# A recurrence's attention weights written already transposed, and its gate products in three pieces

## What is computed

```python
def step(h, x_t):
    proj = h @ W
    score = jnp.einsum('bsh,bh->bs', enc_hiddens, proj)
    attn = jax.nn.softmax(score, axis=-1)
    context = jnp.einsum('bs,bsh->bh', attn, enc_hiddens)
    inp = jnp.concatenate([x_t, context], axis=-1)
    gx = inp @ kernel + bias
    gh = h @ recurrent_kernel
    ...
    z = jax.nn.sigmoid(xz + hz)
    r = jax.nn.sigmoid(xr + hr)
    cand = jnp.tanh(xh + r * hh)
    h_new = z * h + (1.0 - z) * cand
```

## Time and profile before

| | |
|---|---|
| median of 3 runs | 3105.05 us (3101.61 to 3105.86) |
| span of the profiled execution | 3108.8 us |
| TensorE busy | 2731.3 us, 88% |
| VectorE busy | 2144.2 us, 69% |
| ScalarE busy | 1712.7 us, 55% |
| GpSimd busy | 995.6 us, 32% |

### The profile page before, as it was taken

One profiled execution on the slowest core, in us unless ns is written; L12 is line 12 of the kernel. 1 busy time (PEld: TensorE's weight loads), 2 busy tenths in 40 slices (PEclk: granted clock), 3 DMA queues, 4 the chain that ended last, 5 costly groups with the idle time before them and its releaser, 6 DMA issues. The chain is left out here.

```text
span 3108.8 us, 131004 instructions
## 1 busy us (share of the span) xinstructions
PE 2731.3 (88%) x54162; PEld 1800.4 (58%) x54163; DVE 2144.2 (69%) x8143; ACT 1712.7 (55%) x5762; POOL 995.6 (32%) x1992
## 2 busy tenths in 40 slices
PE   7999999887877999898999898999989877777768
PEld 4666666575455555565666565666656544444438
DVE  5666666773433888688888688777868766776653
ACT  4666666533443666576766576666657543333322
POOL 2000000230100666355666355555535311000015
PEclk9999999999878999999999999999999999999989
DMA  4000000000011000010000010000001000000013
GB/s 141 5 5 7 5 5 5 11 1 4 16 37 35 7 14 31 3 38 10 11 10 31 3 44 4 10 7 11 27 3 37 4 3 3 3 4 3 4 45 80
DMA packets 41078, 56.49 MB, mean 18 GB/s; under 512 B 6238, under 2 KB 27688, under 8 KB 40360
## 3 DMA queue, kind: packets, MB, share of 16 engines
q1 hardware_dynamic: 36392, 42.46, 4.3%
q0 software_dynamic: 4096, 5.67, 0.9%
HBM read 42.45 MB, written 5.67 MB: 15 GB/s over the span
## 5 line engine op out<-in xcount | busy, mean ns | idle before, releaser
L2183 POOL TENSOR_TENSOR gru_terms<-gru_states,gru_signs 128x8 f32<-128x8 f32 x512 | 104.2, 203 | 1180.9 <-DVE gru_states L2470 1077.7
L2103 ACT ACTIVATE gru_p<-gru_ps_sg,gru_negmax 128x78 f32<-128x78 f32 x512 | 167.5, 327 | 355.6 <-DVE gru_negmax L2439 350.4
L2107 ACT ACTIVATE gru_th_r<-gru_pre_r 128x32 f32<-128x32 f32 x512 | 118.8, 232 | 406.7 <-DVE gru_pre_r L2450 406.7
L1691 PE MATMUL gru_ps_sg<-ctx_gate_w,gru_p_t 128*4 128x64 f32 x12288 | 268.4, 221 | 0.1
L368 ACT ACTIVATE self_probs<-self_sc,self_negmax 128x512 f32<-128x512 f32 x256 | 174.4, 685 | 166.1 <-DVE self_negmax L425 166.1
L1936 PE MATMUL gru_ps_sg<-score_w,gru_states 128*4 128x78 f32 x4096 | 165.5, 234 | 94.3 <-DVE gru_states L2470 93.4
L2159 POOL TENSOR_SCALAR bg_probs<-bg_probs,bg_arsum 128x256 f32<-128x256 f32 (+2 forms) x192 | 241.0, 1255 | 19.0
L2443 DVE STREAM_TRANSPOSE gru_p_t<-gru_p 128x96 f32<-128x96 f32 x512 | 142.7, 279 | 112.1 <-ACT gru_p L2103 111.9
L2439 DVE TENSOR_REDUCE gru_negmax<-gru_ps_sg 128x1 f32<-128x78 f32 x512 | 121.7, 238 | 135.4 <-PE gru_ps_sg L1936 132.0
L1940 PE MATMUL gru_ps_own<-late,gru_states 128*4 128x128 f32 x4096 | 208.7, 276 | 0.0
L1691 PEld LDWEIGHTS gru_ps_sg<-ctx_gate_w,gru_p_t 128*4 128x4 f32 x12288 | 172.9, 86 | 38.4 <-issue 0.3
(11 more groups left out here) (421 smaller groups left out, 7391.5 us busy)
## 6 DMA issues: line engine op xcount, KB each, us to landing
bg_w<-in_moe_w SPq DMA_DIRECT2D x48, 256.0 KB, 2.9
bg_wa<-in_wqkv SPq DMA_DIRECT2D x24, 192.0 KB, 2.3
moe_w<-in_moe_w SPq DMA_DIRECT2D x16, 256.0 KB, 2.9
best_w_sb<-in_ec_w SPq DMA_DIRECT2D x16, 256.0 KB
cross_scratch<-ctab_raw SPq DMA_DIRECT2D x16, 154.0 KB
cross_outs<-cross_scratch POOLq DMA_DIRECT2D x4, 576.0 KB, 6.1
late<-in_late SPq DMA_DIRECT2D x1, 2269.5 KB
self_w_sb<-in_wqkv SPq DMA_DIRECT2D x8, 192.0 KB, 2.4
```

What stands on the lines that cost most here:

```text
L1691: last = pe.matmul(bank[32 * c:32 * c + B, 0:hi - lo], p_t[:, 32 * k:32 * k + B], gate_w[:, k, 96 * c + lo:96 * c + hi], start=k == 0, sto ...
L2103: act.activation(p[:, 0:CTX + 1], ps_s[:, 0:CTX + 1], ACT.Exp, bias=negmax[:, 0:1], accum_out=total[:, 0:1])\
```

## The change

The scores are computed a second time, with keys on partitions and the 12 pairs (chunk of keys, batch) as columns (`ps_t`), onto a mask product that leaves each block of partitions its own batch. The first set of scores is written to all 32 partitions of a batch, and is used only for the maximum. The exponential reads `ps_t` and writes `p_t`, the operand of the gate products, itself; the transposition, the sum of the exponential, `spread` and the products with it go. `gate_w` gets two columns of ones behind the 32 columns of r in each chunk, so that the product for r also gives the sum; its reciprocal is taken after that product. r with the sum, c and z are three groups of products. The wait for the old-state terms and the history copy moves from the last scan to the transposition of z.

With it the background is dealt out anew: TensorE issues all of it in one place, `after_gates`, between the products for z and the next step's x products; the halves of `down` and of the gate biases become one; the x products wait for `pre_z`; there are three fills in a step without background instead of eight. `STAGES` and the offsets are set anew, q/k transposes always go to a half of `bk_out`, and the pieces of ScalarE and VectorE change places around the recurrence's instructions. The output weights of a head pair have their own semaphores (`s_wo`) and are loaded later than its projections.

The diff, cut to its core:

```diff
--- before.py
+++ after.py
+                dve.scalar_tensor_tensor(out=by_chunk[:, :, 0:32], in0=bias[:, :, 0:32], scalar=is_key[:, k:k + 1],
+                                         in1=product[:, :, 0:32], op0=ALU.mult, op1=ALU.add)
+                dve.scalar_tensor_tensor(out=by_chunk[:, :, GATE_C:GATE_ALL], in0=bias[:, :, 32:96], scalar=is_key[:, k:k + 1],
+                                         in1=product[:, :, 32:96], op0=ALU.mult, op1=ALU.add)
+                dve.tensor_copy(by_chunk[:, :, 32:GATE_C], is_key[:, k:k + 1].rearrange("p (a b) -> p a b", a=1).broadcast_to([P, 4, 2]))
...
-        ps_sg, ps_own, ps_tz = pb("ps_sg"), pb("ps_own"), pb("ps_tz")
-        ps_s, ps_g, ps_t, ps_z = ps_sg[:, 0:P], ps_sg[:, P:2 * P], ps_tz[:, 0:P], ps_tz[:, P:2 * P]
...
+        ps_sr, ps_tc, ps_oz = pb("ps_sr"), pb("ps_tc"), pb("ps_oz")
+        ps_s, ps_r, ps_total = ps_sr[:, 0:CTX + 1], ps_sr[:, P:P + GATE_C], ps_sr[:, P + 32:P + 33]
+        ps_t, ps_c = ps_tc[:, 0:3 * B], ps_tc[:, P:P + 32]
+        ps_own, ps_z = ps_oz[:, 0:P], ps_oz[:, P:P + 32]
...
+        STAGES = {2: {"project": 0, "squares": 0, "take_v": 1, "sums": 1, "scales": 1, "rows": 2, "turn": 2, "take_qk": 4, "scores": 5,
+                      "max0": 6, "exp0": 6, "max1": 7, "exp1": 7, "scale0": 7, "scale1": 8, "probs0": 7, "probs1": 8, "turned0": 7, "turned1": 9,
+                      "values": 9, "take_out": 10, "out": 10, "add": 11},
+                  3: {"project": 0, "squares": 0, "take_v": 1, "sums": 1, "scales": 1, "rows": 2, "turn": 2, "take_qk": 4, "scores": 4,
+                      "max0": 5, "exp0": 5, "max1": 6, "exp1": 6, "scale0": 6, "scale1": 7, "probs0": 7, "probs1": 8, "turned0": 8, "turned1": 9,
+                      "values": 9, "take_out": 10, "out": 11, "add": 12}}
...
-        STAGES = {2: {"project": 0, "squares": 1, "scales": 1, "rows": 2, "turn": 2, "scores": 3, "max0": 4, "exp0": 4, "max1": 5, "exp1": 5,
-                      "scale0": 5, "scale1": 6, "probs0": 6, "probs1": 7, "values": 8, "out": 9, "add": 10},
-                  3: {"project": 0, "squares": 1, "scales": 2, "rows": 3, "turn": 3, "scores": 4, "max0": 5, "exp0": 5, "max1": 6, "exp1": 6,
-                      "scale0": 6, "scale1": 7, "probs0": 7, "probs1": 8, "values": 8, "out": 9, "add": 10}}
...
-                        last = pe.matmul(bank[32 * c:32 * c + B, 0:hi - lo], p_t[:, 32 * k:32 * k + B],
-                                         gate_w[:, k, 96 * c + lo:96 * c + hi], start=k == 0, stop=k == 2,
+                        last = pe.matmul(bank[32 * c:32 * c + B, 0:hi - lo], p_t[:, B * k:B * k + B],
+                                         gate_w[:, k, GATE_ALL * c + lo:GATE_ALL * c + hi], start=k == 0, stop=k == 2,
...
-                for j in (2 * half, 2 * half + 1):
+                for j in range(B):
...
             def turn_qk(g, n, m):
                 pe.wait_ge(s_rows, m + 1)
-                if PACE[g] == 2:
-                    wait_positive(pe, s_add, m - 3)
-                else:
-                    wait_positive(pe, s_apte, 2 * (m - 2) + 2)
-                    wait_positive(pe, s_xt, turned)
+                wait_positive(pe, s_aq, m)
+                wait_positive(pe, s_oe, min(m - 3 if PACE[g] == 2 else m - 2, g * U))
+                if n < 4:
+                    wait_positive(pe, s_add, (g - 1) * U)
...
-            def after_own(t):
-                busy = False
-                for g, n, m in chunks_at(t, 4):
-                    down(g, n, m, 1)
-                    busy = True
-                for g, n, m in units_at(t, "turn"):
-                    turn_qk(g, n, m)
-                    busy = True
-                for j in range(2):
-                    for g, n, m in units_at(t, f"probs{j}"):
-                        turn_probs(g, n, m, j)
-                        busy = True
...
-                if not busy:
-                    wait_positive(pe, s_prez, t)
-                    fill_in(2 * P, ps_tz)
-
-            def before_scores(t):
+            def after_gates(t):
                 busy = False
                 for g, n, m in chunks_at(t, 0):
                     up(g, n, m)
                     busy = True
                 for g, n, m in chunks_at(t, 3):
-                    down(g, n, m, 0)
+                    down(g, n, m)
+                    busy = True
+                for g, n, m in units_at(t, "turn"):
+                    turn_qk(g, n, m)
                     busy = True
                 for g, n, m in units_at(t, "project"):
                     project(g, n, m)
...
                     busy = True
+                for j in range(2):
+                    for g, n, m in units_at(t, f"probs{j}"):
+                        turn_probs(g, n, m, j)
+                        busy = True
...
             for t in range(S):
-                if t:
-                    pe.wait_ge(s_own, t)
+                busy = t and after_gates(t - 1)
+                wait_positive(pe, s_prez, t)
                 wait_positive(pe, s_xt, t // P)
                 for c in range(4):
                     pe.matmul(ps_own[32 * c:32 * c + B, 0:96], x_t[:, B * t:B * (t + 1)], x_w[:, c, :], start=True, stop=False,
                               tile_position=(0, 32 * c), skip_group_check=True)
-                busy = t and before_scores(t - 1)
-                wait_positive(pe, s_u, t)
-                pe.matmul(ps_s[:, 0:CTX + 1], mask_l, mask_r[:, 0:CTX + 1], start=True, stop=False, skip_group_check=True)
+                pe.matmul(ps_t, mask_l, mask_r, start=True, stop=False, skip_group_check=True)
                 if not busy:
-                    wait_positive(pe, s_prez, t)
-                    for i in range(6):
-                        fill_in(2 * P, ps_tz)
+                    for i in range(3):
+                        fill_in(2 * P, ps_sr)
                 pe.wait_ge(s_h, t + 1)
                 for b in range(B):
-                    last = pe.matmul(ps_s[32 * b:32 * b + B, 0:CTX + 1], state(t), score_w[:, b, 0:CTX + 1], start=False, stop=True,
-                                     tile_position=(0, 32 * b), skip_group_check=True)
+                    last = pe.matmul(ps_s[32 * b:32 * b + 32, :], state(t)[:, b:b + 1].broadcast_to([P, 32]), score_w[:, b, 0:CTX + 1],
+                                     start=True, stop=True, tile_position=(0, 32 * b))
                 last.then_inc(s_score, 1)
+                for k in range(3):
+                    for b in range(B):
+                        last = pe.matmul(ps_t[32 * b:32 * b + 32, B * k:B * k + B], score_w[:, b, 32 * k:32 * k + 32], state(t),
+                                         start=False, stop=True, tile_position=(0, 32 * b), skip_group_check=True)
+                last.then_inc(s_turnedmm, 1)
                 for c in range(4):
-                    last = pe.matmul(ps_own[32 * c:32 * c + B, 0:P], state(t), h_w[:, c, :], start=False, stop=True,
+                    last = pe.matmul(ps_own[32 * c:32 * c + B, :], state(t), h_w[:, c, :], start=False, stop=True,
                                      tile_position=(0, 32 * c), skip_group_check=True)
                 last.then_inc(s_ownmm, 1)
-                after_own(t)
                 pe.wait_ge(s_exp, t + 1)
-                for c in range(4):
-                    last = pe.matmul(ps_t[32 * c:32 * c + B, 0:2], spread, total[:], start=True, stop=True, tile_position=(0, 32 * c))
-                last.then_inc(s_total, 1)
+                gate_products(ps_r, 0, GATE_C).then_inc(s_rmm, 1)
+                gate_products(ps_c, GATE_C, GATE_Z).then_inc(s_cmm, 1)
                 pe.wait_ge(s_own, t + 1)
-                fill_in(P, ps_own)
-                pe.wait_ge(s_pt, t + 1)
-                gate_products(ps_g, 0, 64).then_inc(s_rcmm, 1)
-                pe.wait_ge(s_rt, t + 1)
-                gate_products(ps_z, 64, 96).then_inc(s_zmm, 1)
+                gate_products(ps_z, GATE_Z, GATE_ALL).then_inc(s_zmm, 1)
...
                 act.wait_ge(s_max, t + 1)
-                act.activation(p[:, 0:CTX + 1], ps_s[:, 0:CTX + 1], ACT.Exp, bias=negmax[:, 0:1], accum_out=total[:, 0:1])\
-                   .then_inc(s_exp, 1)
+                act.wait_ge(s_turnedmm, t + 1)
+                act.activation(p_t[:], ps_t, ACT.Exp, bias=negmax[:, 0:1]).then_inc(s_exp, 1)
...
+                        add_out(g, n, m)
+                for j in range(2):
+                    for g, n, m in units_at(t, f"max{j}"):
+                        maximum(g, n, m, j)
...
             for t in range(S):
                 before_maximum(t)
                 dve.wait_ge(s_score, t + 1)
-                dve.tensor_reduce(negmax[:], ps_s[:, 0:CTX + 1], axis=AX.X, op=ALU.max, negate=True).then_inc(s_max, 1)
+                dve.tensor_reduce(negmax[:], ps_s[:, 0:CTX], axis=AX.X, op=ALU.max, negate=True).then_inc(s_max, 1)
+                after_maximum(t)
                 dve.wait_ge(s_ownmm, t + 1)
```

(60 more changed lines are left out.)

141 lines of the change are left out of this document (60 added, 81 removed).

## The result

The changed kernel takes 3158.14 us (median of 4 runs, 3152.97 to 3167.19) against 3105.45 us (4 runs, 3101.61 to 3110.28) on the same chip: ratio 1.0179, 95% interval 1.0153 to 1.0204. It is 53 us slower; forecast were 93 us less, and the measured time lies outside the range (2920 to 3120).

What follows compares the result with a forecast made beforehand. Quiet steps were taken as bounded by the recurrence's chain, busy ones by TensorE's order. Tail -77 and +3, attention 3 -14, attention 2 +8, attention 1 -5, experts +4, remaining steps -13, setup +1: 3105 - 93 = 3012 us, range 2920 to 3120.

Steps and rivals of the forecast that it cites:

- The chain, part by part: Step without background, followed from the start of the score products: 3.76 falls by 0.55 to 3.21 us.
- (a): Scores to exponential: the 12 new turned products hide under the maximum; exponential starts at 0.69 us, against 0.66 today.
- (c): Gate products to pre_r: serial reciprocal costs 0.27, narrower first product gives 0.16 back; pre_r at 1.58 us; candidate's products cost nothing.
- The busy step: Steps with background, bounded by TensorE's order: with all background in one place, period 2.01 us plus the background's time.
- Rival 1: Turned products: 32-column loads run serially, exponential 0.44 us later in every step, +225, total 3237 us; chance 0.11.
- (b): Exponential on 12 columns instead of 78 takes 0.21 us; gate products at 0.95, against 1.44 today.
- (d): Last wait before the state scan: 0.04 instead of 0.14 us after the candidate's transposition, 0.10 saved.
- Expert step: Step with expert background: period 3.95 us against 3.91, +0.04.
- W: TensorE's time for the background in a busy step, between z and the next x products; 1.94 us with experts.
- Attention 2: Steps of the second background attention: 4.31 us with scores, 3.95 with projections, mean 4.13 against 4.01, +0.12.
- rival 2: Background steps: waits once met in two windows meet in one, +0.3 us a step, +99, total 3111 us; chance 0.12.
- Rival 4: Steps without background: fewer fills lower TensorE's granted clock, 0.3 us more a step, +42, total 3054 us; chance 0.15.

Runs made afterwards that it cites:

- experiment 2: Kernel before plus 24 unread small products a step where TensorE waits for the exponential: 3297.97 us; control with 3 fills instead: 3136.8; kernel before 3096.21.
- experiment 6: Changed kernel with candidate and z joined in one product, r with total apart: 3025.37 us, ratio 0.9734; also with the earlier background schedule: 2979.19, 0.959.
- experiment 1: Changed kernel with r, total and candidate as one product: 3071.62 us, ratio to the kernel before 0.9912; second run with z joined too: 3117.45, 1.0066.
- old schedule: Background placed as in the kernel before, half of it between own-state and gate products; on the changed kernel with candidate and z joined: 2979.19 us, ratio 0.959.
- the kernel with the fewest instructions: Changed kernel with r, total, candidate and z as one product 98 wide: 3117.45 us, ratio to the kernel before 1.0066.
- old schedule, three products: Changed kernel with the background schedule of the kernel before, r, candidate and z still three products: 3141.29 us, ratio to the kernel before 1.0136.

## Why the prediction was wrong

**The step that failed** is "The chain, part by part", (a) and (c), and with them "The busy step": I priced the new products by their columns and loads, against TensorE's busy time, and found them hidden; I did not count TensorE's instructions as something that has a rate. A step of 3.21 us with 248 of them asks for a packet every 3.31 us (3.21 x 256 / 248), and about 3.75 is what it gets. The view was there: the page's row of q8, 430 packets for TensorE's 108325 loads and products, in the tail 67 of them in 366.2 us, one per 5.47. None of my rivals had it. The Trainium skill (Runtime: NRT & Kernel Launch, Instruction fetch mechanics) says that each engine refills its instruction memory in blocks of 16 KiB, 256 instructions, while it executes, and that this stays hidden because instructions are dispatched slower than they are fetched. The blocks are as it says; that they stay hidden the trace refutes here, where the step asks for one per 3.31 us: by that rule the forecast would not have lacked this term, and in experiment 2 unread instructions lengthen a tail in which they fit into TensorE's wait.

With 48 instructions a step taken out and nothing else but the order of z (experiment 6), the time is 3025.37 against the forecast 3012, and most periods lie beside the forecast ones: attention 3 3.71 (3.67), attention 1 3.74 (3.78), experts 4.00 (3.95); tail 3.35 (3.21) and attention 2 4.26 (4.13) stay above. The supply and what z waited for cost the change (1.0179 - 0.9734) x 3105 = 138 us of the 146 that it missed the forecast by. These two were taken away together. In the tail and in attention 1 and 3 it is the supply: with z left as it was, experiment 1 has 3.77 and 3.76 in these two (4.03 and 4.09 in the changed kernel). In the expert steps it is z: they stay at 4.13 with r and c joined, and fall to 4.00 here and to 3.98 with all joined, the two kernels of this schedule in which z does not wait for the own copy.

By its own points:
- (a) Exponential at 0.69: right to the hundredth, and it waits for the maximum. Rival 1 (serial narrow loads) is refuted: 24 loads and products of 32 columns take 0.35. (The 0.112 a load that the prediction reads from the earlier trace rows is 2.75 / 24 = 0.115; nothing hangs on it.)
- (b) The exponential on 12 columns took 0.27, not 0.21, gate products at 1.02: term undersized by 0.07 a step. That is 10 us over the tail's 140 steps.
- (c) Gates to pre_r took 0.65 (1.02 to 1.67), forecast 0.63: right where no packet is waited for. "The candidate's products cost nothing" is the part that fell: 48 instructions.
- (d) The scan starts 0.06 after the transposition has ended (2990.16 to 2990.22): 0.08 saved, 0.10 forecast.
- **Expert step.** TensorE of the kernel after:

```profile
1858.29 0.34 PE L1932 MATMUL gru_ps_sr<-score_w,gru_states 128*32 128x78 f32 x8
...
1858.85 0.68 DVE L2193 SCALAR_TENSOR_TENSOR bg_hid<-gru_bg_turn,bg_u 128x512 f32<-128x512 f32 x1
...
1859.31 0.37 PE L1705 MATMUL gru_ps_sr<-ctx_gate_w,gru_p_t 128*4 128x34 f32 x24 [0.25 <-ACT gru_p_t L2100]
1859.45 0.28 DVE L2431 COPY gru_own<-gru_ps_oz 128x128 f32<-128x128 f32 x1
...
1859.79 0.36 PE L1705 MATMUL gru_ps_oz<-ctx_gate_w,gru_p_t 128*4 128x32 f32 x24
1860.07 1.13 PE L1721 MATMUL gru_bg_in<-h_cols,bg_w 128*128 128x512 f32 x2
1861.04 1.05 PE L1733 MATMUL gru_bg_pair<-bg_w,bg_hid 128*128 128x128 f32 x8
1862.02 0.35 PE L1924 MATMUL gru_ps_oz<-late,x_t 128*4 128x96 f32 x8
```

  Next scores at 1862.41: 4.12 for a forecast of 3.95. Of the 0.17, 0.07 is (b) and 0.12 is z, which starts 0.48 behind r (0.36 forecast): it waits for the own copy, ended at 1859.73, and that stands behind the hidden-layer product (L2193). I had seen that product delay "the reciprocal" and missed that z stands behind the copy. W was right (1.95 for 1.94).
- **Attention 2**, the step with scores, kernel after:

```profile
1575.17 0.37 PE L1705 MATMUL gru_ps_sr<-ctx_gate_w,gru_p_t 128*4 128x34 f32 x24 [0.25 <-ACT gru_p_t L2100]
...
1575.39 0.58 ACT L2027 ACTIVATE bg_probs<-gru_bg_pair,bg_amax 128x384 f32<-128x384 f32 x1
...
1575.85 0.21 ACT L2027 ACTIVATION_READ_ACCUMULATOR bg_probs<-gru_bg_pair,bg_amax 128x1 f32 x1
1576.16 0.92 PE L1766 MATMUL gru_bg_pair<-keys,bg_q 64*128 64x384 f32 x4 [0.18 <-issue]
```

  From r to the background scores 0.99 for a forecast of 0.65: they overwrite the bank that the second exponential of the unit before still reads, until 1576.06, in this same step, and the program has a wait for it (the profile gives "issue" here, so the cause is read from the program and the times). That is rival 2's mechanism, at a place that I had not named. This step takes 4.75 (4.31 forecast), the one with projections 3.79 (3.95). That the old schedule brings attention 2 from 4.26 to 3.92 in experiment 6 fits, but it moves more than this one wait; which part is its own was not tried.
- Attention 1 and 3 were forecast faster (3.78, 3.67) and came out at 4.03 and 4.09; with c and z joined they are at 3.74 and 3.71. Their excess goes with the 48 instructions.
- Rival 4 (clock): in the kernel after the tail's granted clock is 0.96 against 0.99. Ten of the 97 steps lie below full clock and take 0.4 more than the others: some 4 us. In the kernel with the fewest instructions it costs 0.21 a step.
- The total of experiment 6, 13 us over the forecast, is near it partly by luck: the quiet step is 0.14 too long (20 us over 140 steps) and attention 2 0.13 (8 us), so other steps must have given some of it back; which, I did not work out.

## What to carry to other kernels

Count instructions beside columns: an fp32 product of TensorE is four of them in these traces, and where many small products replace one wide one, compare the new number a step with what the instruction queue delivers (here 256 per 3.75 us) before costing their time. If TensorE shows "issue" gaps of half a microsecond inside a burst that waits for nothing, look at the instruction queue's packets in the DMA view. Join narrow products that read the same operand, the first-needed one apart (here r with the total; candidate with z), and keep background work where the engine would wait anyway.

## What the runs showed of the hardware

- Instructions of TensorE come in packets of 16 KB, about 256 instructions, on a queue of their own (q8), and never faster than one per 3.70 us on average over some 100 steps, in four kernels with 248 to 296 a step, with the DMA engines otherwise idle (share 0.02). What sets this pace (the packet itself takes 0.88 to 1.5 us) no run here shows; nor whether the other engines' instructions (q14) bear on it. The shortest distance of two packets in the tails is 3.22 us (old schedule, three products).
- Where the supply is short, the period is not steady: 3.32 to 4.13 in the tail of the kernel after, 3.75 to 6.32 in the kernel before with 24 more products.
- The granted clock differed with what filled the step, and moved in stretches: 0.88 with 152 instructions a step (steps of 4.57 instead of 3.63), 0.98 with 200, 1.00 when three fills are added, but 0.82 with 296 under a TensorE that waits for its instructions.
- Loads of 32 columns for four column tiles overlap: 24 loads and 24 products in 0.35 us; one after another at the 0.028 us of the prediction the loads alone would take 0.67.
